# Down projection with the activations as the stationary operand, in a fused attention, routing and expert FFN kernel

## What is computed

```python
base1 = t @ w1.T
base3 = t @ w3.T
h1 = base1[None] + SCALING * einsum('etr,efr->etf', einsum('td,erd->etr', t, a1), b1)
h3 = base3[None] + SCALING * einsum('etr,efr->etf', einsum('td,erd->etr', t, a3), b3)
act = silu(h1) * h3
out_e = einsum('etf,df->etd', act, w2) + SCALING * einsum('etr,edr->etd', einsum('etf,erf->etr', act, a2), b2)
out = einsum('te,etd->td', weights, out_e)
x = x + out
```

## Time and profile before

| | |
|---|---|
| time, median of 3 runs | 1376.12 us (1375.61 to 1377.21) |
| the profiled execution | 1376.15 us, its span 1374.3 us |
| instructions | 17227 |
| TensorE matmuls | busy 1334.7 us, 97% |
| TensorE weight loads | busy 1122.3 us, 82% |
| VectorE | busy 870.2 us, 63% |
| ScalarE | busy 543.3 us, 40% |
| GpSimd | busy 222.9 us, 16% |
| mean granted TensorE clock | 0.997 of full speed |

### The profile page before, as it was taken

The page is one execution under the profiler, slowest core; times in us unless marked ns, Lnnn a source line. Parts: engine busy times, 40 slices in busy tenths (PEclk is TensorE's granted clock), DMA queues, the critical chain, the costliest instruction groups (busy, mean ns, idle before and its releaser), DMA issues.

```text
span 1374.3 us, 17227 instructions
## 1 busy us (share of the span) xinstructions
PE 1334.7 (97%) x6660; PEld 1122.3 (82%) x6660; DVE 870.2 (63%) x1552; ACT 543.3 (40%) x1039; POOL 222.9 (16%) x171
## 2 busy tenths in 40 slices
PE   7999999999999999999999999999999999999997
PEld 7999997878787878787878878787878787878785
DVE  6787656756666567656765567566765676565654
ACT  5877773423333333333333334332433333332332
POOL 2333350201001111102020202020110111020200
PEclk9999999999999999999999999999999999999998
DMA  8344621020101011101101020201010111110000
GB/s 272 121 140 143 204 87 31 2 70 1 54 17 39 31 39 31 40 31 32 38 12 59 1 69 2 69 1 55 16 44 26 39 32 40 31 39 31 1 16 15
DMA packets 59321, 69.47 MB, mean 51 GB/s; under 512 B 7002, under 2 KB 46312, under 8 KB 58984
## 3 DMA queue, kind: packets, MB, share of 16 engines
q1 hardware_dynamic: 59216, 68.38, 16.2%
q10 hardware_dynamic: 24, 0.01, 0.0%
HBM read 51.27 MB, written 17.10 MB: 50 GB/s over the span
## 4 chain that ended last, share of the span: by engine, by line
PE 88%; issue 6%; DVE 4%; ACT 1%; POOL 1%; DMA 0%; POOLq 0%; ACTq 0%; DVEq 0%
PE bank L1075 27%; PE bank L1077 27%; PE bank L1076 26%; PE bank L1121 2%; PE bank L1171 2%; PE bank L1149 1%; PE bank L1177 1%; PE bank L1271 1%; DVE act_b L977 1%; DVE z_a L1003 1%; DVE z_b L999 1%; ACT z_hi L675 1%; DVE z_a L1000 1%; PE bank L1114 1%; DVE z_lo L1005 1%
## 5 line engine op out<-in xcount | busy, mean ns | idle before, releaser
L969 DVE TENSOR_TENSOR act_a<-silu_a,bank 128x512 f32<-128x512 f32 x128 | 87.9, 687 | 217.8 <-PE bank L1077 201.2
L669 ACT ACTIVATE s_hi<-act_s 128x512 fp32r<-128x512 f32 x128 | 80.9, 632 | 259.4 <-DVE act_s L984 259.4
L990 DVE TENSOR_TENSOR s_lo<-act_s,s_hi 128x512 fp32r<-128x512 f32 x128 | 102.7, 802 | 75.4 <-ACT s_hi L669 74.2
L662 ACT ACTIVATE silu_b<-bank 128x512 f32<-128x512 f32 x128 | 76.0, 594 | 162.4 <-PE bank L1077 161.0
L977 DVE TENSOR_TENSOR act_b<-silu_b,bank 128x512 f32<-128x512 f32 x128 | 87.9, 687 | 63.0 <-PE bank L1077 61.9
L658 ACT ACTIVATE silu_a<-bank 128x512 f32<-128x512 f32 x128 | 76.0, 594 | 126.3 <-PE bank L1077 125.4
L1075 PE MATMUL bank<-t_hi,w1T_hi 128*128 128x512 f32 x256 | 102.2, 399 | 22.3 <-DVE act_b L977 22.3
L538 POOL TENSOR_TENSOR v_lo<-v_full,v_hi 128x512 fp32r<-128x512 f32 x64 | 94.6, 1510 | 128.9 <-ACT v_hi L654 128.9
L984 DVE TENSOR_TENSOR act_s<-act_a,act_br 128x512 f32<-128x512 f32 x128 | 103.2, 807 | 4.4
L522 POOL TENSOR_TENSOR t_lo<-t_scaled,t_hi 128x1024 fp32r<-128x1024 f32 x16 | 38.5, 2404 | 414.9 <-ACT t_hi L650 414.9
L1077 PE MATMUL bank<-s_hi,w2T_lo 128*128 128x512 f32 x256 | 100.6, 393 | 0.0
(11 more groups left out here) (175 smaller groups left out, 3160.4 us busy)
## 6 DMA issues: line engine op xcount, KB each, us to landing
x_in<-in_x SPq DMA_DIRECT2D x32, 256.0 KB, 3.0
kv<-in_fside_BxSxS SPq DMA_DIRECT2D x32, 256.0 KB, 3.2
t_scratch<-oT SPq DMA_DIRECT2D x32, 256.0 KB, 2.1
t_in<-t_scratch SPq DMA_DIRECT2D x16, 512.0 KB
x_out<-in_x SPq DMA_DIRECT2D x16, 512.0 KB, 3.9
out<-x_out SPq DMA_DIRECT2D x32, 256.0 KB, 2.2
rho<-scale_scratch SPq DMA_DIRECT2D x16, 256.0 KB
rstd<-scale_scratch SPq DMA_DIRECT2D x16, 256.0 KB
```

Source lines behind the costliest of these rows:

```text
L662: nc.scalar.activation(silu_b[:, :], h1_bank[j % 2][:, :], ACT.Silu).then_inc(silu_b_ready, 1)
L669: nc.scalar.activation(s_hi[j % 2][:, :], act_s[j % 2][:, :], ACT.Copy).then_inc(s_hi_ready, 1)
L969: nc.vector.tensor_tensor(act_a[j % 2][:, :], silu_a[j % 2][:, :], h3_bank[j % 2][:, :], ALU.mult).then_inc(act_a_ready, 1)
L990: nc.vector.tensor_tensor(s_lo[j % 2][:, :], act_s[j % 2][:, :], f32(s_hi[j % 2][:, :]), ALU.subtract)
```

## The change

The stationary and the moving operand of the down projection change places. `down_y` loads 128 tokens of `s_hi` or `s_lo` as the stationary operand and moves the 256 columns of w2 over it, for four blocks of tokens: 12 matmuls of 256 columns instead of 6 of 512, into the halves of the same two banks. `finish_y` does the same with z and b2, and signals `y_ready` twice, once for each bank. y is then token by token: `transpose_y`, both copies and `yT` are gone; `scale_y` and `add_residual` read `y_bank`, one chunk earlier than before (in chunk 2 instead of 3). TensorE waits in `wait_y_read` for both before it writes y of the new tile, and in chunk 4 no longer waits for them.

`down_z(c-1, 7)` moves behind `second_expert(c, 0)` and `down_y(c-1, 7)`, so both last products stand behind the next tile's chunk 0; `mask_z` waits for `down_done` and moves behind `second_act(c, 0)`, `z_high` behind `down_high(c, 0)`. In the last tile VectorE does both halves of the residual. `rt` is allocated with the lasting buffers.

```diff
             def scale_y(c):
-                act.wait_ge(yT_ready, 2 * c + 1)
+                act.wait_ge(y_ready, 2 * c + 2)
                 act.wait_ge(rt_ready, c + 1)
                 for k in range(KT // 2, KT):
-                    last = nc.scalar.activation(y_scaled[:, k - KT // 2, :], h3_bank[0][:, (k % 2) * D:(k % 2 + 1) * D],
+                    last = nc.scalar.activation(y_scaled[:, k - KT // 2, :], y_bank[1][:, (k % 2) * D:(k % 2 + 1) * D],
                                                 ACT.Copy, scale=rt[c % 2][:, k:k + 1])
...
                     first_silu(c, j)
-                    if j == 1 and not first:
-                        z_high(c - 1)
                     if j == 2 and not first:
-                        copy_y0(c - 1)
+                        scale_y(c - 1)
                     second_silu(c, j - 1)
-                    if j == 3 and not first:
-                        scale_y(c - 1)
...
                     down_high(c, j - 1, buffer_used=not (first and j < 3))
+                    if j == 1 and not first:
+                        z_high(c - 1)
...
-            def mask_z(c):
+            def mask_z(c, last=False):
                 n = c + 1
-                dve.wait_ge(z_in_ready, n)
+                if last:
+                    dve.wait_ge(z_in_ready, 1)
+                else:
+                    dve.wait_ge(down_done, chunk_no(c, FC))
...
+            def add_residual(c, half, ready):
+                dve.wait_ge(y_ready, 2 * c + half + 1)
                 dve.wait_ge(x_loaded[c % 2], 16 * (c // 2 + 1))
-                for k in range(KT // 2):
-                    last = nc.vector.scalar_tensor_tensor(x_out[c % 2][:, k, :], h1_bank[0][:, k * D:(k + 1) * D],
+                for h in range(KT // 2):
+                    k = half * KT // 2 + h
+                    last = nc.vector.scalar_tensor_tensor(x_out[c % 2][:, k, :], y_bank[half][:, h * D:(h + 1) * D],
...
                     first_act(c, j)
+                    if j == 2 and not first:
+                        add_residual(c - 1, 0, out_a_ready)
+                    second_act(c, j - 1)
                     if j == 1 and not first:
                         mask_z(c - 1)
-                    if j == 2 and not first:
-                        copy_y1(c - 1)
-                    second_act(c, j - 1)
-                    if j == 3 and not first:
-                        add_residual(c - 1)
...
-            mask_z(end)
-            copy_y1(end)
-            add_residual(end)
+            mask_z(end, last=True)
+            add_residual(end, 0, out_a_ready)
+            dve.wait_ge(out_b_ready, end)
+            add_residual(end, 1, out_b_ready)
...
+            def y_block(k):
+                return y_bank[k // 2][:, k % 2 * D:(k % 2 + 1) * D]
+
             def down_y(c, j):
                 pe.wait_ge(down_in_ready, chunk_no(c, j) + 1)
-                for half in range(DC):
-                    last = product(y_bank[half][:, :], at(w2T, ALL, j, slice(half * P, (half + 1) * P)),
-                                   (s_hi[j % 2][:, :], s_lo[j % 2][:, :]), j == 0, False)
+                for k in range(KT):
+                    last = product(y_block(k), at((s_hi[j % 2], s_lo[j % 2]), ALL, slice(k * P, (k + 1) * P)),
+                                   at(w2T, ALL, j), j == 0 and k % 2 == 0, False, grouped=False)
...
             def finish_y(c):
                 pe.wait_ge(z_lo_ready, c + 1)
-                for half in range(DC):
-                    last = product(y_bank[half][:, :], at(b2T, ALL, slice(half * P, (half + 1) * P)),
-                                   (z_hi[:, :], z_lo[:, :]), False, True)
-                last.then_inc(y_ready, 1)
...
+                for k in range(KT):
+                    last = product(y_block(k), at((z_hi, z_lo), ALL, slice(k * P, (k + 1) * P)),
+                                   at(b2T, ALL, ALL), False, True, grouped=False)
+                    if k % 2 == 1:
+                        last.then_inc(y_ready, 1)
+
+            def wait_y_read(c):
+                pe.wait_ge(out_a_ready, c + 1)
+                pe.wait_ge(y_scaled_ready, c + 1)
...
-                    if j == 4 and not first:
-                        pe.wait_ge(out_a_ready, c)
-                        pe.wait_ge(y_scaled_ready, c)
-                    elif not (first and j == 1):
+                    if not (first and j == 1):
                         pe.wait_ge(act_b_ready, n + j - 1)
                     first_expert(c, j)
-                    if j == 1 and not first:
-                        down_z(c - 1, FC - 1).then_inc(z_in_ready, 1)
                     if j == 2 and not first:
                         finish_y(c - 1)
                     second_expert(c, j - 1)
                     if j == 1 and not first:
-                        down_y(c - 1, FC - 1).then_inc(down_done, 1)
+                        down_y(c - 1, FC - 1)
+                        down_z(c - 1, FC - 1).then_inc(down_done, 1)
...
                         down_z(c, 0)
                         if not first:
-                            wait_y_copied(c - 1)
+                            wait_y_read(c - 1)
                         down_y(c, 0).then_inc(down_done, 1)
                     elif j == 3:
                         down_y(c, 1)
-                        if not first:
-                            pe.wait_ge(act_b_ready, n + 3)
-                            transpose_y(c - 1)
                         down_z(c, 1).then_inc(down_done, 1)
...
             finish_y(end)
-            pe.wait_ge(act_b_ready, chunk_no(end, FC))
-            wait_y_copied(end)
-            transpose_y(end)
```

More of the change, by code:

```diff
@@ L111, in adaln_moe_ffn @@
         neg_max = [sb(ctx, f"neg_max{k}", [P, SC]) for k in range(2)]
+        rt = [sb(ctx, f"rt{k}", [P, KT]) for k in range(2)]
         early = ExitStack()
@@ L170, in adaln_moe_ffn @@
         z_lo = sb(late, "z_lo", [ER, TILE], F32R)
-        yT = sb(late, "yT", [P, DC, TILE])
         y_scaled = sb(late, "y_scaled", [P, KT // 2, D])
-        rt = [sb(late, f"rt{k}", [P, KT]) for k in range(2)]
         x_out = [sb(late, f"x_out{k}", [P, KT, D]) for k in range(2)]
@@ L256, in adaln_moe_ffn @@
         y_ready = sem("y_ready")
-        y0_copied = sem("y0_copied")
-        y1_copied = sem("y1_copied")
-        yT_ready = sem("yT_ready")
         y_scaled_ready = sem("y_scaled_ready")
@@ L564, in _ @@
             add_residual(TILES - 2)
-            add_residual(TILES - 1)
         @block.scalar
@@ L675, in z_high @@
                 nc.scalar.activation(z_hi[:, :], z_a[:, :], ACT.Copy).then_inc(z_hi_ready, 1)
-            def copy_y0(c):
-                act.wait_ge(y_ready, c + 1)
-                nc.scalar.activation(yT[:, 0, :], y_bank[0][:, :], ACT.Copy).then_inc(y0_copied, 1)
             def scale_y(c):
-                act.wait_ge(yT_ready, 2 * c + 1)
+                act.wait_ge(y_ready, 2 * c + 2)
                 act.wait_ge(rt_ready, c + 1)
                 for k in range(KT // 2, KT):
-                    last = nc.scalar.activation(y_scaled[:, k - KT // 2, :], h3_bank[0][:, (k % 2) * D:(k % 2 + 1) * D],
+                    last = nc.scalar.activation(y_scaled[:, k - KT // 2, :], y_bank[1][:, (k % 2) * D:(k % 2 + 1) * D],
                                                 ACT.Copy, scale=rt[c % 2][:, k:k + 1])
@@ L731, in _ @@
             z_high(end)
-            copy_y0(end)
-            act.wait_ge(out_b_ready, end)
-            scale_y(end)
         @block.vector
@@ L1005, in mask_z @@
                 nc.vector.tensor_tensor(z_lo[:, :], z_a[:, :], f32(z_hi[:, :]), ALU.subtract).then_inc(z_lo_ready, 1)
[L1007 to L1013, removed]
+            def add_residual(c, half, ready):
+                dve.wait_ge(y_ready, 2 * c + half + 1)
                 dve.wait_ge(x_loaded[c % 2], 16 * (c // 2 + 1))
-                for k in range(KT // 2):
-                    last = nc.vector.scalar_tensor_tensor(x_out[c % 2][:, k, :], h1_bank[0][:, k * D:(k + 1) * D],
+                for h in range(KT // 2):
+                    k = half * KT // 2 + h
+                    last = nc.vector.scalar_tensor_tensor(x_out[c % 2][:, k, :], y_bank[half][:, h * D:(h + 1) * D],
                                                           rt[c % 2][:, k:k + 1], x_out[c % 2][:, k, :],
                                                           ALU.mult, ALU.add)
-                last.then_inc(out_a_ready, 1)
+                last.then_inc(ready, 1)
             def dve_tile(c, first=False, last=False, routes=False):
```

## The result

| | before | after |
|---|---|---|
| time, median of 4 runs | 1375.86 us (1375.03 to 1377.21) | 1357.37 us (1357.17 to 1357.85) |
| span of the profiled execution | 1374.3 us | 1355.3 us |
| one tile without routing work, start to start | 72.63 us | 71.5 us |

The ratio is 0.9865, with an interval of 0.9848 to 0.9882. The change makes the kernel 18.5 us faster. The forecast was 34.1 us faster, and its range ended at 1354: the time lies 15.4 us above the forecast and outside the range.

What follows compares the result with a forecast made beforehand. The prediction took TensorE, busy 97% of the span, as the bound, with one hole at each tile boundary. From 1376.15 us, -25.5 - 13.2 + 7.8 - 3.2 = -34.1 gave 1342.0 us, range 1337 to 1354.

Steps and rivals of the forecast that it cites:

- Part 1: Tile boundaries: TensorE's 1.68 us standstill behind `act_b` goes in tiles 1 to 15, -25.5 us.
- part 5: Tail after the last `z_lo`: without copies and transposes the last store leaves earlier, -3.2 us (bounds -2.2 and -3.7).
- The tight place: Before `finish_y` in chunk 2: `z_lo` would be ready only 0.2 us before TensorE wants to load it.
- Part 2: Other engines' waits for y and `z_lo`: nothing on TensorE's path; without the cover, 1.2 us a tile and more.
- Part 3: `down_y` and `finish_y`: 12 short matmuls at 0.119 us replace 6 long, +0.055 us a group, +7.8 us in all.
- The 0.083 us for entering and leaving: Possible cost per group of switching between long and short matmuls, at most +11.7 us in all; taken as 0.
- the one row: Attention-stage row with 512 columns after 256: 0.31 us behind it, 0.08 too much, put down to its own wait.
- Part 4: Transposes of y: eight transposes cost 0.88 us a tile; removing them in 15 tiles gives -13.2 us.
- A: Before `finish_y`: a slowed `mask_z` makes `z_lo` late, 0.66 us in 15 tiles, +9.9 us, 1351.9; chance 0.11.
- B: Switches between long and short matmuls: 0.083 us each time, +11.7 us, 1353.7; chance 0.15.
- C: Short matmuls: the 846 added weight loads are not hidden, some 0.11 us each, +93 us, 1427 us; chance 0.05.
- D: Chunk 1's second half: the hole only moves there, TensorE again losing 1.68 us, 1367.6 us; chance 0.03.

Runs made afterwards that it cites:

- old addresses: Changed kernel with `rt` back behind the other buffers and an unused buffer where `yT` lay, so buffers lie as before the change: 1335.84 us.
- 4032 bytes added: Changed kernel with an unused buffer of 4032 bytes behind `rt`, ahead of the working buffers, weights unmoved: 1335.35 us.
- experiment 4: Changed kernel with unused buffers putting working buffers at distance 0 from the weights, but 64 bytes from w2 and b2: 1330.4 us.

## Why the prediction was wrong

**Part 1, the hole, was right.** -25.5 us forecast. The order of z alone gives -26.9 against its own runs of before (1375.28). The two traces differ by 28.1 us: 14 x 1.71 and, with the longest wait, 2.0 in the last tile make 26.0 in the tiles. The other 2.1 are scatter between executions: 0.8 ahead of the tiles, whose first starts between 194.2 and 195.3 us in the fourteen traces, and 1.2 in the tail, for the reason given at part 5. The tight place held as well: `z_lo` ended 0.5 us before `finish_y`.

**Part 2, no new wait, was right.** No wait behind `x_out` or `y_scaled` is among TensorE's.

**Part 3, the short matmuls, was mis-sized in both directions.** It took their pitch from the attention stage, 0.119. But that stage reads other buffers at other distances, and its own pitch stays between 0.119 and 0.120 in all fourteen kernels. That fits the distance too: every shift moves both of its operands together. At the old addresses the group takes 1.386 us, +0.013 over six long ones: 141 x 0.013 = +1.8 us where +7.8 stood. At the new ones it takes 1.431 to 1.438, about 1 us in all over the forecast. The 0.083 us for entering and leaving are not there: in after 0.23 us follow the first long matmul behind a short group, so taking the one row for its own wait was right. The Trainium skill ("TensorE: Matmul & The Clock Gate", "Back-to-back issue gap") with N/2.4 + 2.5 ns gave an estimate of +2 us for this part, and the old addresses show +1.8. They agree only in the difference: its 216 and 109 ns for one matmul are met by no run, the lowest means are 226.7 and 115.5.

**Part 4, the transposes, was right**, as the 0.76 us a tile above shows. **Part 5, the tail, was right** at -3.2 us: from `finish_y` to the end of the span there were 9.6 us and are 6.5. The way there was different, the low bound for the matmuls and less for the rest. The end of after:

```profile
1348.82 0.58 PE L1060 MATMUL bank<-b2T_hi,z_hi 128*128 128x256 f32 x1 [2.13 <-DVE z_lo L995]
...
1351.33 0.41 PE L1062 MATMUL bank<-b2T_hi,z_lo 128*128 128x256 f32 x1
1350.50 0.88 DVE L1002 SCALAR_TENSOR_TENSOR x_out<-bank,rt,x_out 128x256 f32<-128x256 f32 x2 [1.74 <-PE bank L1062]
1351.84 0.88 DVE L1002 SCALAR_TENSOR_TENSOR x_out<-bank,rt,x_out 128x256 f32<-128x256 f32 x2 [0.46 <-issue]
```

All of `finish_y` runs at 0.215 us a short matmul behind a wait of 2.13 us of TensorE. The granted clock is 0.50 there, the level of 1.2 GHz (columns: stretch, its length, busy time of each engine, granted clock, DMA share, GB/s):

```profile
1349.00:1352.00 3.00, 2.75 (x12) 2.45 (x12) 1.04 (x3) 0.00 (x0) 0.00 (x0) 0.50 0.00 0
```

Against that the two pairs of VectorE's operations take 0.88 us each and not 2 x 0.48, and follow the matmuls closely. How far the low level reaches into the tail differs from trace to trace. In before it took in the last matmuls of `finish_y` and the eight transposes (1.94 us):

```profile
1366.00:1370.00 4.00, 2.77 (x10) 1.68 (x9) 1.01 (x2) 1.44 (x3) 0.20 (x1) 0.50 0.00 0
```

In the three other traces with the old tail the transposes ran at 1.00 in 1.06 us, and it took 8.4 us; the changed tail took 5.3 in the trace with 4032 bytes added, where all of it ran at 1.00:

```profile
1326.80:1332.00 5.20, 1.63 (x12) 1.44 (x12) 1.66 (x4) 0.00 (x0) 0.00 (x0) 1.00 0.29 101
```

So with the full clock in both, the tail gains 3.1 us as well; a single pair of traces can be off by 1.2.

**The step that failed is one that the prediction did not have.** The sum puts the cost of the 4032 long matmuls at nothing: it treats their pitch of 0.2289 as fixed, and `rt`'s new place as no edit. With part 3 at its measured +1.8 and the other terms as forecast the sum is -25.5 - 13.2 + 1.8 - 3.2 = -40.1 us, and 1376.15 - 40.1 = 1336.0 us, where the changed kernel at the old addresses measures 1335.84. That it comes so close is partly luck: part 1 gave 1.4 us more than its term, the other three together 1.3 us less (-13.3 for -14.6). To this the 64 bytes add 14.5 us in the long matmuls and some 6.5 in the short ones (141 x 0.046), which makes 1357.0 of the 1357.37 measured. So the change is worth 40 us, and one moved allocation in it takes half of that back.

**The rivals.** None of them happened. A: no wait on `z_lo` in a tile. B: see part 3. C: the added loads are hidden, since the pitch stays at 0.120 us or less with loads of 0.19. The Trainium skill's rule in "The mechanism" of the same page, that a load overlaps only matmuls of other row groups, is not borne out by any of these kernels; a sentence ahead of it in that section also lets a load into a background weight buffer go ahead, and that would fit. D: the tile of the kernel with the order of z alone is 1.71 us shorter. That 1357 lies just beyond B's 1353.7 is chance; the forecast's check for B, 0.31 us behind a short group, clears it.

## What to carry to other kernels

When TensorE is busy 97% of the time, its pitch is a term of the sum, and a change that adds, drops or reorders a buffer has moved operands and may change that pitch: here 64 bytes were worth 21 us on 1336. Compare the start-to-start distance of matmuls that the change leaves alone before looking for a cause in the new order. A pitch read in another stage holds for that stage's buffers, so bound it by what the addresses can do, here 3% between the best and the worst distance for each kind.

## What the runs showed of the hardware

- The pitch of a matmul with a new stationary operand depends on the distance, within 256 bytes of a partition, between the operand that is being moved and the one that is being loaded: 226.7 to 233.4 ns for 512 columns, 115.5 to 119.5 ns for 256, with float32r operands. The period rests on two pairs of kernels. That only the distance counts rests on one run that moved both sides and on the attention stage; for 256 columns experiment 4 speaks against it, 117.8 ns at the distance that gave 115.5. The granted clock was 0.998 to 1.000 of full speed in the profiled execution of all these kernels of the after order.
- The best distance differs between the kinds: of those tried, 0 for the long ones and 64 for the short ones.
- The profile shows this nowhere as a wait. Busy time of TensorE is 99% in the kernel at 1357 us and in the one at 1330 us; the counts in a stretch, and the busy time of the weight loads with them, tell them apart. The stretch from 215 to 1300 us (columns as above, matmuls in the first bracket), in after and then in the kernel of experiment 4:

```profile
215.00:1300.00 1085.00, 1085.00 (x5469) 915.72 (x5468) 676.26 (x1141) 370.85 (x642) 144.81 (x90) 1.00 0.11 32
```

```profile
215.00:1300.00 1085.00, 1085.00 (x5596) 932.36 (x5595) 688.26 (x1159) 377.33 (x654) 144.49 (x90) 1.00 0.11 32
```

  5469 against 5596 matmuls, 2.3% more, at the same busy time of the matmuls and the same clock.
